# One DMA issue per image of f, earlier copies of images 0 and 1, and one f pair and the attention product ahead of the first taps, in a fused convolution and attention kernel

## The chip, the cores and the metric

The kernel runs on one core of one Trainium2 chip. The metric is the device time of one execution in microseconds (us). Five engines work side by side on a core, each through its own queue in order: TensorE (PE in the profile; its weight loads are PEld), VectorE (DVE), ScalarE (ACT), GpSimd (POOL) and SyncE (SP), which here issues nearly all DMA transfers. They wait for one another through semaphores.

## The reference

For x of 16 images with 256 channels of 32 x 32 pixels, in float32:

```python
x = x + conv_block(_gn(x))      # _gn: group norm, 32 groups of 8 channels
x = x + attention(_gn(x))

# conv_block, cut
f  = relu(einsum('nchw,oc->nohw', x, cw) + conv_b)                  # 256 -> 64 channels
g  = relu(einsum('nc,oc->no', x.mean((2, 3)), cw) + conv_b)         # same weights on the pixel means
K_img = g[:, :, None] * wk + conv_kernel_b                          # 5 x 5 taps per image and channel
gk = relu(k_w0 * K_img + k_w1 * K_img.mean(0) + k_b)                # likewise gk2, 3 x 3
y1 = depthwise_conv(f, gk) + adap_bias                              # 5 x 5
y2 = depthwise_conv(f, gk2, dilation 2) + atrous_bias               # 3 x 3
out = einsum('nchw,oc->nohw', concat(y1, y2), fuse_w) + fuse_b      # 128 -> 256 channels

# attention: blocks of 8 x 8 with a halo of 4; every key that lies inside the image is masked with the
# same large negative number, so a block whose 16 x 16 window lies inside gets the mean of its values
```

What is left of the attention for this input shape is small: the four inner 8 x 8 blocks of every image get one vector, the mean over a 16 x 16 window of the normalised x times Wv and Wout; the outer blocks get the output bias alone.

## The kernel before

All 16 images of x stay in SBUF (tile `xs`). The work goes in two stages that overlap.

**Stage 1, batches of four images.** SyncE loads x, one issue per image (line 202). DVE and ACT compute channel sums, TensorE averages them over groups (`groups(k)`, line 703), DVE and POOL turn that into a reciprocal deviation per channel (`power`, line 301), and POOL multiplies it into the 1x1 weights (`scaled_weights(k)`, line 310). DVE's `scale(k)` (lines 547 to 555) makes the shifts and the pixel means `gm`. TensorE's `f_pair(q)` (line 723) multiplies images 2q and 2q+1 with them, 32 matmuls for two pairs, so 16 for one; ACT's `store_f(q)` (lines 424 to 432, four activations) adds the bias, applies relu and writes f into a slot in SBUF, as 64 channels of eight planes of 153 words. SyncE writes f to a DRAM scratch `fd` (`write_f`, line 214), in four issues per image, each with every fourth channel.

**Stage 2, one image at a time.** SyncE reads each image back from `fd` into one of two buffers `fc[n % 2]`, three copies shifted by one word (`copies(n)`, line 223; 32 rows each); it waits for the image's write and for the taps that used that buffer. TensorE's `taps(n, h)` (line 785, two halves of 32 matmuls) convolves both kernels at once, with weights `wbuf[n % 2]` that POOL (lines 329, 332) and ACT (line 442, four activations per image) make from the scales. DVE transposes the result and orders it (lines 642, 654), TensorE's `fuse(n, c)` (line 797) multiplies it with the fusion weights, DVE adds it to x (line 660), and ACT squares it for the second norm. Chains of two to four images then compute the window means and the inner vectors; POOL adds them and SyncE stores the rows.

**Between the stages**, on TensorE in this order: the first half of f pair 5; a wait for the pixel means `gm`, then the g product (line 746); the second half of f pair 5; two products that spread the scales over the 96 rows of the taps (lines 752, 755), each behind DVE's masked scales (line 609); the bias product (line 757); `shifts(3)` (line 709); and, behind the load of its weights, the attention product Wv by Wout (line 762). DVE copies the spread scales out (lines 616, 629), makes image 0's taps (lines 620 to 626) and finishes the fusion bias (line 631). Then `taps(0)` starts, when copies(0) has landed; f pairs 6 and 7 come between taps(0) and taps(1).

**What sets the order.** Every engine's queue is written out by hand; nothing is scheduled. SyncE's runs: x; the attention weights (lines 205, 207) into `fc[1]`, which is free until copies(1); the writes of images 0 to 5; copies(0); images 6 and 7; a wait for the attention product and the spread scales, which read `fc[1]`; copies(1); images 8 and 9; then per image n copies(n + 2) and, for n below 3, two more writes; from n = 6 on the stores. The slots of f and the odd weight buffer lie in the same tile `reg`, so `taps(1)` on ACT waits until images 4 and 5 are written. PSUM banks are shared too: pairs 0 and 3, the attention product, the spread scales and pair 7 use `pf[0]`; pairs 1, 4 and 6 use `pf[1]`; pairs 2 and 5 use the bank of the odd taps halves.

Of the kernel before, what the change touches and what calls it, by code (L numbers as in the profile page):

```python
# [9 lines left out]
ACT = mybir.ActivationFunctionType  # L10
AX = mybir.AxisListType

N, C, H, W = 16, 256, 32, 32
# [51 lines left out]
def build(nc, x, cw_t, columns, wkv, wout_t, out):  # L65
    with ExitStack() as ctx:
        def sb(name, shape, dt=F32):
            return ctx.enter_context(nc.sbuf_tensor(name, shape, dt))
# [8 lines left out]

        xs = sb("xs", [128, N * NC2 * HW])
        fc = [sb(f"fc{b}", [128, COPY]) for b in range(2)]
        reg = sb("reg", [128, 3072 + WALL])  # L80
        yt = reg[:, 0:1024]
        y2 = [reg[:, 1024:2048], reg[:, 2048:3072]]
        wa = sb("wa", [128, WALL])
# [15 lines left out]
        yb, mixv = cst[:, COLS["yb"]], cst[:, COLS["mix"]]  # L99
        sel, mask16 = cst[0:64, COLS["sel"]], cst[0:64, COLS["mask16"]]  # L100
        wkc, bkc, onc, mask4 = (cst[0:KROWS, COLS[k]] for k in ("wk", "bk", "on", "mask4"))
        wv, wot = fc[1][:, 0:512], fc[1][:, 512:1024]
        sx = fc[1][0:64, 1024:1536].rearrange("p (n g v) -> p n g v", n=N, v=2)

        sm = sb("sm", [128, 622])
        cut = [0]
# [92 lines left out]
        @block.sync  # L199
        def _(sp):  # L200
            for n in range(N):
                sp.dma_start(xs[:, n * NC2 * HW:(n + 1) * NC2 * HW].rearrange("p (c f) -> p c f", c=NC2),  # L202
                             x_v[:, n * NC2:(n + 1) * NC2, :]).then_inc(s_x[n], 16)
            sp.wait_ge(s_fcz, 2)
            sp.dma_start(wv.rearrange("p (k c) -> p k c", k=2),  # L205
                         wkv[C:2 * C, :].rearrange("(k p) c -> p k c", p=128)).then_inc(s_attw, 16)
            sp.dma_start(wot.rearrange("p (k o) -> p k o", k=2),  # L207
                         wout_t.rearrange("(k p) o -> p k o", p=128)).then_inc(s_attw, 16)

            def write_f(n):  # L210
                sp.wait_ge(s_fev, n // 2 + 1)
                m = 64 * (n % 2)
                for c4 in range(4):
                    sp.dma_start(bass.AP(fd, n * IMG + c4 * SPLIT * SET, [[PLANE, GROUPS], [SET, SPLIT], [1, PLANE]]),  # L214
                                 slots[n // 2][m + c4:m + c4 + 61:4, :].rearrange("p (h f) -> p h f", h=SPLIT)
                                 ).then_inc(s_fw[n], 16)

            def copies(n):
                sp.wait_ge(s_fw[n], 64)
                if n >= 2:  # L220
                    sp.wait_ge(s_tap, 2 * (n - 2) + 2)
                for k in range(3):
                    sp.dma_start(fc[n % 2][32 * k:32 * k + 32, LEAD - k:LEAD - k + RUN],  # L223
                                 bass.AP(fd, n * IMG, [[SET, 32], [1, RUN]])).then_inc(s_cp[n % 2], 16)

            def store_rows(n, r0, r1):
                src = xs[:, n * NC2 * HW:(n + 1) * NC2 * HW].rearrange("p (c f) -> p c f", c=NC2)
                sp.dma_start(out_v[:, n * NC2:(n + 1) * NC2, r0 * W:r1 * W],
                             src[:, :, r0 * W:r1 * W]).then_inc(s_store, 16)

            def outer(n):
# [12 lines left out]
            for n in range(6):  # L244
                write_f(n)
            copies(0)
            write_f(6)
            write_f(7)
            sp.wait_ge(s_smm, 2)
            sp.wait_ge(s_atm, 1)  # L250
            copies(1)
            write_f(8)
            write_f(9)
            for n in range(N):
                if n + 2 < N:
                    copies(n + 2)
                if n < 3:
                    write_f(10 + 2 * n)
                    write_f(11 + 2 * n)
                if 6 <= n < 14:  # L260
                    whole(n - 6)
                if n in (12, 13):
                    outer(n - 4)
                if n == 14:
                    inner_rows(8)
                    inner_rows(9)
                    outer(12)
                if n == 15:
                    whole(10)
                    whole(11)  # L270
# [12 lines left out]
        @block.gpsimd  # L283
        def _(pool):
# [17 lines left out]

            def scaled_weights(k):
                pool.wait_ge(s_rstd, k + 1)
                if k == 0:
                    pool.wait_ge(s_cw, 16)
                if k >= 2:
                    pool.wait_ge(s_fmm, 2 * (k - 1))
                r = rstds[k % 2].rearrange("p (j c) -> p j c", c=NC2)
                pool.tensor_tensor(wsc[k % 2], cw[:, :, 0:CM].unsqueeze(2).to_broadcast([128, NC2, BATCH, CM]),  # L310
                                   r.rearrange("p j c -> p c j").unsqueeze(3).to_broadcast([128, NC2, BATCH, CM]),
                                   ALU.mult).then_inc(s_wsc, 1)
# [90 lines left out]
        def _(act):  # L403
# [30 lines left out]
            def taps(n):  # L434
                act.wait_ge(s_pre, n)
                if n == 1:
                    act.wait_ge(s_fw[4], 64)
                    act.wait_ge(s_fw[5], 64)
                if n >= 2:
                    act.wait_ge(s_tap, 2 * (n - 2) + 2)  # L440
                for c4 in range(4):
                    ins = act.activation(wchannel(n, c4), taps_of(n), ACT.Relu, scale=mask4[:, c4:c4 + 1])  # L442
                ins.then_inc(s_w, 1)
# [34 lines left out]
            x_sums(2, 2)  # L478
            for u in range(4):
                x_sums(3, u)  # L480
            for q in range(2, 6):
                store_f(q)
            act.wait_ge(s_p0, 1)
            for c4 in (3,):
                ins = act.activation(wchannel(0, c4), taps_of(0), ACT.Relu, scale=mask4[:, c4:c4 + 1])
            ins.then_inc(s_w0, 1)
            act.wait_ge(s_atm, 1)
            act.activation(at[:, :], pf[0][:, 0:HALF], ACT.Copy, scale=1.0 / KEYS).then_inc(s_at, 1)
            taps(1)
            store_f(6)  # L490
            store_f(7)
            for n in range(1, N):
                if n + 1 < N:
# [13 lines left out]
        def _(dve):  # L507
# [126 lines left out]
            def transpose_half(n, h):  # L634
                i = 2 * n + h
                dve.wait_ge(s_tap, i + 1)
                if n == 0:
                    dve.wait_ge(s_fw[0], 64)
                    dve.wait_ge(s_fw[1], 64)
                else:  # L640
                    dve.wait_ge(s_y2, n)
                dve.transpose(yt[:, h * HALF:(h + 1) * HALF], pt[i % 3]).then_inc(s_t1, 1)  # L642

            def order_image(n):
                dve.wait_ge(s_t1, 2 * n + 2)
                if n < 2:
                    for q in range(2, 6):
                        dve.wait_ge(s_fw[q], 64)
# [48 lines left out]
        def _(pe):  # L697
# [43 lines left out]
            f_pair(4)  # L741
            groups(3)
            f_pair(5, (0,))
            pe.wait_ge(s_gm, BATCHES)
            for c in range(NC2):
                mm = pe.matmul(px[:, 64:64 + N], cw[:, c, :], gm[:, c, :], start=(c == 0), stop=(c == NC2 - 1))
            mm.then_inc(s_gmm, 1)
            f_pair(5, (1,))

            pe.wait_ge(s_sx, 1)  # L750
            flat = fc[1][0:64, 1024:1536]
            pe.matmul(px[0:KROWS, 0:64], sel, flat[:, 0:64], start=True, stop=True).then_inc(s_smm, 1)
            pe.wait_ge(s_sx, 2)
            pe.wait_ge(s_fev, 4)
            pe.matmul(pf[0][0:KROWS, HALF + 64:HW], sel, flat[:, 64:512], start=True, stop=True).then_inc(s_smm, 1)
            for c in range(NC2):
                pe.matmul(pt0[:, 96 + c:97 + c], fw[:, 128 * c:128 * (c + 1)], yb, start=True, stop=True)
            shifts(3)
            pe.wait_ge(s_attw, 32)
            for c in range(NC2):  # L760
                for e in range(NC2):
                    mm = pe.matmul(pf[0][:, C * c:C * (c + 1)], wv[:, C * e + 128 * c:C * e + 128 * (c + 1)],
                                   wot[:, C * e:C * (e + 1)], start=(e == 0), stop=(e == NC2 - 1))
            mm.then_inc(s_atm, 1)

            def taps(n, h):
                i = 2 * n + h
# [53 lines left out]
            for n in range(N):  # L821
# [5 lines left out]
                    if n == when + 1:  # L827
                        attention(k)
                if n == 0:
                    f_pair(6)  # L830
                    f_pair(7)
                else:
                    fuse(n - 1, 0)
                    fuse(n - 1, 1)
# [66 lines left out]
```

## Time and profile before

| | |
|---|---|
| median of 3 runs | 208.42 us (208.18 to 208.69) |
| profiled execution | 209.72 us |
| its span, first to last instruction | 207.6 us |
| mean granted TensorE clock | 0.967 |
| busy share of the span: PE, DVE, ACT, POOL | 79%, 72%, 60%, 43% |
| mean DMA rate | 264 GB/s |

A busy share is an average over stages with different limits. The chain of waits is followed back from the last instruction: at each step to what released it, or to the instruction before it on its engine. PE times are modelled at their ends, and a row of a timeline can merge several instructions (x8). "idle before" names what ended the wait. The granted clock is a share of full speed, 1.00 being 2.4 GHz and 0.50 being 1.2 GHz.

### The profile page before, as it was taken

How to read it: one execution, taken by the hardware profiler on the slowest of the kernel's cores; microseconds unless marked ns; L12 is line 12 of the kernel's file. 1: busy time of each engine (PE TensorE's matmuls, PEld its weight loads, DVE VectorE, ACT ScalarE, POOL GpSimd, SP SyncE). 2: the span in 40 equal slices, each digit the busy share in tenths (PEclk: the TensorE clock that was granted, in tenths of full speed). 3: DMA queues.
4: the chain of work that ended last, by engine and by line, in shares of the span. 5: the costliest groups of instructions: out<-in, count | busy, mean ns of one | idle time of the engine just before them, and what ended most of it. 6: DMA issues, size and time to landing. Idle time of an engine off the chain costs nothing.

```text
span 207.6 us, 3885 instructions
## 1 busy us (share of the span) xinstructions
PE 163.5 (79%) x1374; PEld 102.6 (49%) x1374; DVE 150.1 (72%) x336; ACT 125.2 (60%) x235; POOL 90.1 (43%) x145
## 2 busy tenths in 40 slices
PE   0001796966676999999999999999999999999230
PEld 0000332322246555875775775686676577575030
DVE  0298949887670507898989789989789899799611
ACT  2766679979155064956775775685585686445500
POOL 8703205041339004044146577338857427537540
PEclk9999999999996999999999999999999999999955
DMA  6999999999598996899548487987989998863996
GB/s 218 406 410 410 408 410 410 409 380 213 133 207 190 222 227 161 196 209 222 126 106 184 108 282 180 309 276 186 307 279 253 273 350 211 334 244 153 376 362 223
DMA packets 24466, 54.82 MB, mean 264 GB/s; under 512 B 2560, under 2 KB 14592, under 8 KB 22912
## 3 DMA queue, kind: packets, MB, share of 16 engines
q1 hardware_dynamic: 24032, 54.14, 85.4%
q10 hardware_dynamic: 416, 0.44, 0.8%
q8 instruction: 11, 0.18, 0.4%
q14 instruction: 7, 0.06, 0.1%
HBM read 32.78 MB, written 21.79 MB: 263 GB/s over the span
## 4 chain that ended last, share of the span: by engine, by line
PE 63%; SPq 26%; DMA 4%; DVE 2%; issue 2%; POOL 1%; DVEq 0%; ACT 0%; POOLq 0%
PE pt L785 29%; PE pf L797 28%; SPq L202 14%; SPq L214 9%; DMA fc<-fd 4%; PE pf L723 3%; PE px L817 3%; SPq L207 2%; DVE bs L669 1%; DVE xs L181 1%; DVE xs L660 1%; PE px L808 1%; POOL cw L363 0%; SPq L223 0%; SPq L205 0%
## 5 line engine op out<-in xcount | busy, mean ns | idle before, releaser
L451 ACT ACTIVATE junkt<-xs,sm 128x1024 bf16<-128x1024 f32 x32 | 36.8, 1149 | 39.6 <-DVE xs L660 39.6
L797 PE MATMUL pf<-reg,cst 128*128 128x512 f32 x128 | 59.0, 604 | 0.0
L660 DVE SCALAR_TENSOR_TENSOR xs<-pf,cst,xs 128x1024 f32<-128x1024 f32 x32 | 40.7, 1273 | 8.2 <-PE pf L797 8.2
L642 DVE STREAM_TRANSPOSE reg<-pt 128x512 f32<-128x512 f32 x32 | 22.9, 716 | 20.5 <-PE pt L785 14.3
L329 POOL TENSOR_TENSOR pre<-cst,sv 96x512 f32<-96x512 f32 x15 | 15.8, 1053 | 47.1 <-ACT wa L442 23.1
L418 ACT ACTIVATE wa<-xs 128x1024 bf16<-128x1024 f32 x28 | 29.3, 1051 | 10.6 <-DMA xs<-x_dram 10.6
L797 PEld LDWEIGHTS pf<-reg,cst 128*128 128x128 f32 x128 | 23.0, 190 | 24.4 <-issue 24.4
L785 PE MATMUL pt<-fc,wa 96*64 96x128 f32 x512 | 31.4, 283 | 3.0 <-DMA fc<-fd 3.0
L785 PEld LDWEIGHTS pt<-fc,wa 96*64 96x64 f32 x512 | 29.5, 142 | 8.8 <-issue 5.3
L785 PEld LDWEIGHTS pt<-fc,reg 96*64 96x64 f32 x512 | 27.9, 136 | 5.9 <-issue 5.9
L785 PE MATMUL pt<-fc,reg 96*64 96x128 f32 x512 | 29.7, 273 | 0.0
L181 POOL TENSOR_TENSOR xs<-xs,sm 128x128 f32<-128x128 f32 x58 | 21.3, 401 | 9.7 <-ACT sm L468 9.7
L723 PE MATMUL pf<-xs,junkt 128*64 128x512 f32 x96 | 23.6, 638 | 0.0
L669 DVE TENSOR_REDUCE bs<-xs 128x9 f32<-128x576 f32 x32 | 23.2, 731 | 0.0
L654 DVE STREAM_TRANSPOSE reg<-reg 128x256 f32<-128x256 f32 x64 | 22.8, 414 | 0.5
L520 DVE BATCH_NORM_STATS2 sm<-xs 128x6 f32<-128x512 f32 x36 | 22.5, 681 | 0.2
L442 ACT ACTIVATE reg<-pre,cst 96x512 f32<-96x512 f32 x32 | 21.2, 744 | 1.2 <-POOL pre L332 1.2
L301 POOL TENSOR_TENSOR sm<-sm 128x8 f32<-128x8 f32 x4 | 6.6, 1640 | 33.7 <-DVE sm L545 33.7
L332 POOL TENSOR_TENSOR pre<-pre,sm 96x512 f32<-96x512 f32 x15 | 19.3, 1286 | 1.2
L442 ACT ACTIVATE wa<-pre,cst 96x512 f32<-96x512 f32 x28 | 18.6, 744 | 0.0
L703 PE MATMUL px<-sm,cst 128*128 128x16 f32 x8 | 1.8, 297 | 19.2 <-DVE sm L537 19.2
L723 PEld LDWEIGHTS pf<-xs,junkt 128*64 128x64 f32 x96 | 6.9, 147 | 12.3 <-issue 12.2
(88 smaller groups left out, 125.9 us busy)
## 6 DMA issues: line engine op xcount, KB each, us to landing
xs<-x_dram SPq DMA_DIRECT2D x16, 1024.0 KB, 18.8
fc<-fd SPq DMA_DIRECT2D x48, 306.0 KB, 5.3
out_dram<-xs SPq DMA_DIRECT2D x10, 1024.0 KB, 6.0
out_dram<-xs SPq DMA_DIRECT2D x12, 256.0 KB, 4.3
out_dram<-xs SPq DMA_DIRECT2D x6, 512.0 KB, 3.4
fd<-own SPq DMA_DIRECT2D x40, 76.5 KB, 5.3
fd<-reg SPq DMA_DIRECT2D x24, 76.5 KB, 4.7
cst<-columns_dram ACTq DMA_DIRECT2D x1, 304.0 KB, 4.0
```

The source lines that it names most:

```text
L181: ins = engine.tensor_tensor(rows, rows, add.to_broadcast([128, 8, 2, 8]), ALU.add)
L202: sp.dma_start(xs[:, n * NC2 * HW:(n + 1) * NC2 * HW].rearrange("p (c f) -> p c f", c=NC2), x_v[:, n * NC2:(n + 1) * NC2, :]).then_inc(s_x ...
L418: act.activation(junkl[m % 2], plane(n, c), func, scale=scale, accum_out=dst).then_inc(s_xs, 1)
L442: ins = act.activation(wchannel(n, c4), taps_of(n), ACT.Relu, scale=mask4[:, c4:c4 + 1])
L451: act.activation(junk[m % 2], plane(n, c), ACT.Square, bias=nwb[:, c:c + 1], accum_out=accq[:, 1, m:m + 1]).then_inc(s_sq, 1)
L642: dve.transpose(yt[:, h * HALF:(h + 1) * HALF], pt[i % 3]).then_inc(s_t1, 1)
L654: ins = dve.transpose(dst[:, k], src[:, k])
L660: dve.scalar_tensor_tensor(out=plane(n, c), in0=pf[c][:, :], scalar=fb[:, c:c + 1], in1=plane(n, c), op0=ALU.add, op1=ALU.add, accum_out=r ...
L669: dve.reduce_sum(bs[:, 9 * (m % 16):9 * (m % 16) + 9].rearrange("p (a b) -> p a b", a=3), src, AX.XY).then_inc(s_bs, 1)
L723: mm = pe.matmul(fbank[q][parts, h * HALF:(h + 1) * HALF], wsc[k % 2][:, c, 2 * p + m, :], plane(2 * q + m, c)[:, h * HALF:(h + 1) * HALF] ...
L785: mm = pe.matmul(pt[i % 3][64 * j:64 * j + 64, 128 * s:128 * s + 128], wgroup(n, g, r), rhs, start=(r == 0), stop=(r == 1), tile_position= ...
L797: mm = pe.matmul(pf[c][:, h * HALF:(h + 1) * HALF], fw[:, 128 * c:128 * (c + 1)], y2[n % 2][:, h * HALF:(h + 1) * HALF], start=True, stop= ...
```

## The change

- **f writes.** Each image is written in one issue of 64 channels by eight planes in place of four issues. For that the 64 channels are put in another order on the host (`perm`, applied to the 1x1 weights and biases), and the masks `mask4`, `mask16` and `sel` follow it. The waits on a written image go from 64 to 16.
- **Buffers.** The attention weights and the masked scales move from `fc[1]` to free columns of `reg`, which grows by 96 words; ACT's taps(1), which overwrites them there, waits for the second spread product.
- **SyncE's order.** Images 0 to 3, the two weight loads, copies(0), copies(1), images 4 to 13, copies(2), images 14 and 15, and from there as before. The wait for the attention product and the spread scales ahead of copies(1) is gone.
- **TensorE's order.** First half of pair 5, attention product (with its waits), g product, shifts(3), bias product, first spread, second half of pair 5, second spread, pair 6, taps(0), pair 7, taps(1).
- **ACT's order.** After pair 4's store come the attention matrix, the fourth channel of image 0's taps, the stores of pairs 5 and 6, taps(1), and the store of pair 7.
- **POOL.** The last `scaled_weights` waits until DVE has all pixel means.

```diff
-        wv, wot = fc[1][:, 0:512], fc[1][:, 512:1024]
-        sx = fc[1][0:64, 1024:1536].rearrange("p (n g v) -> p n g v", n=N, v=2)
+        wv, wot = reg[:, 3672:4184], reg[:, 4184:4696]
+        sx = reg[0:64, 4696:5208].rearrange("p (n g v) -> p n g v", n=N, v=2)
...
-                for c4 in range(4):
-                    sp.dma_start(bass.AP(fd, n * IMG + c4 * SPLIT * SET, [[PLANE, GROUPS], [SET, SPLIT], [1, PLANE]]),
-                                 slots[n // 2][m + c4:m + c4 + 61:4, :].rearrange("p (h f) -> p h f", h=SPLIT)
-                                 ).then_inc(s_fw[n], 16)
+                sp.dma_start(bass.AP(fd, n * IMG, [[PLANE, CM], [CM * PLANE, SPLIT], [1, PLANE]]),
+                             slots[n // 2][m:m + CM, :].rearrange("p (h f) -> p h f", h=SPLIT)).then_inc(s_fw[n], 16)
...
-            for n in range(6):
+            for n in range(4):
                 write_f(n)
+            sp.dma_start(wv ...)      # the two weight loads, from ahead of the writes
+            sp.dma_start(wot ...)
+            sp.wait_ge(s_fcz, 2)
             copies(0)
-            write_f(6)
-            write_f(7)
-            sp.wait_ge(s_smm, 2)
-            sp.wait_ge(s_atm, 1)
             copies(1)
-            write_f(8)
-            write_f(9)
+            for n in range(4, 14):
+                write_f(n)
             for n in range(N):
                 if n + 2 < N:
                     copies(n + 2)
-                if n < 3:
-                    write_f(10 + 2 * n)
-                    write_f(11 + 2 * n)
+                if n == 0:
+                    write_f(14)
+                    write_f(15)
...
             def scaled_weights(k):
                 pool.wait_ge(s_rstd, k + 1)
+                if k == BATCHES - 1:
+                    pool.wait_ge(s_gm, BATCHES)
...
                 if n == 1:
-                    act.wait_ge(s_fw[4], 64)
-                    act.wait_ge(s_fw[5], 64)
+                    act.wait_ge(s_fw[4], 16)
+                    act.wait_ge(s_fw[5], 16)
+                    act.wait_ge(s_smm, 2)
...
-            for q in range(2, 6):
+            for q in range(2, 5):
                 store_f(q)
+            act.wait_ge(s_atm, 1)
+            act.activation(at[:, :], pf[0][:, 0:HALF], ACT.Copy, scale=1.0 / KEYS).then_inc(s_at, 1)
             act.wait_ge(s_p0, 1)
...
             ins.then_inc(s_w0, 1)
-            act.wait_ge(s_atm, 1)
-            act.activation(at[:, :], pf[0][:, 0:HALF], ACT.Copy, scale=1.0 / KEYS).then_inc(s_at, 1)
+            store_f(5)
+            store_f(6)
             taps(1)
-            store_f(6)
             store_f(7)
...
             f_pair(5, (0,))
+            pe.wait_ge(s_attw, 32)
+            pe.wait_ge(s_fev, 4)
+            (attention product)
             pe.wait_ge(s_gm, BATCHES)
             (g product)
-            f_pair(5, (1,))
-            (first spread, second spread, bias product)
             shifts(3)
-            pe.wait_ge(s_attw, 32)
-            (attention product)
+            (bias product, first spread)
+            f_pair(5, (1,))
+            (second spread)
+            f_pair(6)
...
                 if n == 0:
-                    f_pair(6)
                     f_pair(7)
```

## Rows read from the trace of the kernel before

**Rows 1.** The page: its span, and the chain that ended last by engine.

```profile
span 207.6 us, 3885 instructions
...
PE 63%; SPq 26%; DMA 4%; DVE 2%; issue 2%; POOL 1%; DVEq 0%; ACT 0%; POOLq 0%
```

**Rows 2.** The chain in order of time: start us, us, what.

```profile
55.40 0.58 SPq L223
...
56.49 7.35 DMA fc<-fd
...
69.27 6.87 PE pf L723 x32
...
79.64 3.63 PE pf L797 x8
83.27 3.65 PE pt L785 x64
...
191.31 1.83 PE pf L797 x4
```

**Rows 3.** Timeline of PE: start us, us, instruction, idle before it.

```profile
50.29 1.94 PE L723 MATMUL pt<-xs,junkt 128*64 128x512 f32 x8
54.30 0.62 PE L746 MATMUL px<-sm,cw 128*128 128x16 f32 x4 [2.07 <-DVE sm L555]
...
56.71 0.38 PE L752 MATMUL px<-fc,cst 64*96 64x64 f32 x2
57.03 0.99 PE L755 MATMUL pf<-fc,cst 64*96 64x448 f32 x2
57.95 0.61 PE L757 MATMUL pt<-cst 128*128 128x1 f32 x4
...
58.86 1.97 PE L762 MATMUL pf<-fc 128*128 128x256 f32 x8
63.88 5.38 PE L785 MATMUL pt<-fc,wa 96*64 96x128 f32 x64 [3.05 <-DMA fc<-fd]
```

**Rows 4.** Windows: PE, PEld, DVE, ACT, POOL busy (x), PEclk, DMA share, GB/s.

```profile
46.00:48.00 2.00, 2.00 (x12) 0.57 (x8) 1.94 (x5) 1.94 (x3) 0.00 (x0) 1.00 1.16 301
...
54.00:56.00 2.00, 1.70 (x10) 1.01 (x12) 1.15 (x7) 0.00 (x0) 0.02 (x1) 1.00 0.40 118
...
63.90:67.40 3.50, 3.50 (x36) 3.50 (x38) 0.00 (x0) 1.35 (x3) 3.06 (x3) 0.54 0.95 194
```

**Rows 5.** Timeline of ACT, DVE and POOL before and around the first taps.

```profile
34.07 0.16 DVE L553 TENSOR_TENSOR sm<-sm 128x8 f32<-128x8 f32 x1
...
46.06 1.06 ACT L418 ACTIVATE wa<-xs 128x1024 bf16<-128x1024 f32 x1 [0.39 <-DMA xs<-x_dram]
...
50.65 0.51 ACT L431 ACTIVATE own<-pf,sm 128x256 f32<-128x256 f32 x1
...
52.97 1.05 POOL L310 TENSOR_TENSOR junkt<-cw,sm 128x512 f32<-128x512 f32 x1
53.01 1.03 DVE L553 TENSOR_TENSOR sm<-sm 128x8 f32<-128x8 f32 x1
...
60.02 0.61 DVE L629 COPY sv<-pf 96x448 f32<-96x448 f32 x1
...
61.05 0.16 DVE L631 TENSOR_TENSOR cst<-pt,cst 128x2 f32<-128x2 f32 x1
...
62.62 2.63 ACT L442 ACTIVATE reg<-pre,cst 96x512 f32<-96x512 f32 x4 [1.15 <-POOL pre L332]
```

**Rows 6.** Sources of issues: ns min/median/max; last line, copies to landing.

```profile
L202 SPq DMA_DIRECT2D xs<-x_dram x16: 438/2234/5354, 0.7 to 26.6; - x16
...
L214 SPq DMA_DIRECT2D fd<-reg x24: 597/600/2371, 35.5 to 54.8; - x24
...
L223 SPq DMA_DIRECT2D fc<-fd x48: 302/422/1547, 55.4 to 170.2; - x48
...
DMA to landing us min/median/max: 3.5/5.3/7.3
```

More of the change, by code:

```diff
@@ L79, in build @@
         fc = [sb(f"fc{b}", [128, COPY]) for b in range(2)]
-        reg = sb("reg", [128, 3072 + WALL])
+        reg = sb("reg", [128, 3072 + WALL + 96])
         yt = reg[:, 0:1024]
@@ L203, in _ @@
                              x_v[:, n * NC2:(n + 1) * NC2, :]).then_inc(s_x[n], 16)
[L204 to L208, printed above, removed]
             def write_f(n):
@@ L212, in write_f @@
                 m = 64 * (n % 2)
-                for c4 in range(4):
-                    sp.dma_start(bass.AP(fd, n * IMG + c4 * SPLIT * SET, [[PLANE, GROUPS], [SET, SPLIT], [1, PLANE]]),
-                                 slots[n // 2][m + c4:m + c4 + 61:4, :].rearrange("p (h f) -> p h f", h=SPLIT)
-                                 ).then_inc(s_fw[n], 16)
+                sp.dma_start(bass.AP(fd, n * IMG, [[PLANE, CM], [CM * PLANE, SPLIT], [1, PLANE]]),
+                             slots[n // 2][m:m + CM, :].rearrange("p (h f) -> p h f", h=SPLIT)).then_inc(s_fw[n], 16)
             def copies(n):
-                sp.wait_ge(s_fw[n], 64)
+                sp.wait_ge(s_fw[n], 16)
                 if n >= 2:
@@ L242, in inner_rows @@
                 store_rows(n, IN0, IN1)
-            for n in range(6):
+            for n in range(4):
                 write_f(n)
+            sp.dma_start(wv.rearrange("p (k c) -> p k c", k=2),
+                         wkv[C:2 * C, :].rearrange("(k p) c -> p k c", p=128)).then_inc(s_attw, 16)
+            sp.dma_start(wot.rearrange("p (k o) -> p k o", k=2),
+                         wout_t.rearrange("(k p) o -> p k o", p=128)).then_inc(s_attw, 16)
+            sp.wait_ge(s_fcz, 2)
             copies(0)
-            write_f(6)
-            write_f(7)
-            sp.wait_ge(s_smm, 2)
-            sp.wait_ge(s_atm, 1)
             copies(1)
-            write_f(8)
-            write_f(9)
+            for n in range(4, 14):
+                write_f(n)
             for n in range(N):
@@ L637, in transpose_half @@
                 if n == 0:
-                    dve.wait_ge(s_fw[0], 64)
-                    dve.wait_ge(s_fw[1], 64)
+                    dve.wait_ge(s_fw[0], 16)
+                    dve.wait_ge(s_fw[1], 16)
                 else:
@@ L647, in order_image @@
                     for q in range(2, 6):
-                        dve.wait_ge(s_fw[q], 64)
+                        dve.wait_ge(s_fw[q], 16)
                 else:
@@ L743, in _ @@
             f_pair(5, (0,))
[L744 to L747, printed above, removed]
-            f_pair(5, (1,))
[L750 to L753, printed above, removed]
-            pe.wait_ge(s_fev, 4)
[L755 to L758, printed above, removed]
-            pe.wait_ge(s_attw, 32)
+            pe.wait_ge(s_attw, 32)
+            pe.wait_ge(s_fev, 4)
             for c in range(NC2):
@@ L764, in _ @@
             mm.then_inc(s_atm, 1)
+            pe.wait_ge(s_gm, BATCHES)
+            for c in range(NC2):
+                mm = pe.matmul(px[:, 64:64 + N], cw[:, c, :], gm[:, c, :], start=(c == 0), stop=(c == NC2 - 1))
+            mm.then_inc(s_gmm, 1)
+            shifts(3)
+            for c in range(NC2):
+                pe.matmul(pt0[:, 96 + c:97 + c], fw[:, 128 * c:128 * (c + 1)], yb, start=True, stop=True)
+            pe.wait_ge(s_sx, 1)
+            flat = reg[0:64, 4696:5208]
+            pe.matmul(px[0:KROWS, 0:64], sel, flat[:, 0:64], start=True, stop=True).then_inc(s_smm, 1)
+            f_pair(5, (1,))
+            pe.wait_ge(s_sx, 2)
+            pe.matmul(pf[0][0:KROWS, HALF + 64:HW], sel, flat[:, 64:512], start=True, stop=True).then_inc(s_smm, 1)
+            f_pair(6)
             def taps(n, h):
@@ L853 @@
             for e in range(6):
-                p = 32 * (e // 2) + 8 * c4 + 2 * ph + e % 2
+                p = 32 * (e // 2) + 8 * ph + 4 * (e % 2) + c4
                 mask4[p, c4] = 1.0
@@ L867 @@
     mask16 = np.zeros((128, GROUPS), np.float32)
-    for ch in range(CM):
-        mask16[ch, ch // 4] = 1.0
-        for p in range(KROWS):
-            if p % 32 // 8 == ch % 4:
-                sel[ch, p] = 1.0
+    for q in range(CM):
+        mask16[q, q % GROUPS] = 1.0
+        sel[q, q // GROUPS:KROWS:4] = 1.0
+    perm = 4 * (np.arange(CM) % GROUPS) + np.arange(CM) // GROUPS
     group_mean = (row[:, None] // GROUP == row[None, :] // GROUP).astype(np.float32) / GROUP
@@ L880 @@
                           a["L0_conv_conv_k2_w"].reshape(-1), a["L0_conv_conv_k2_b"]])
-    conv_b = a["L0_conv_conv_b"].reshape(CM, 1)
-    cw_t = a["L0_conv_conv_w"].reshape(CM, C).T
+    conv_b = a["L0_conv_conv_b"][perm].reshape(CM, 1)
+    cw_t = a["L0_conv_conv_w"].reshape(CM, C)[perm].T
     parts = {"gmat": group_mean, "fw": fw_t, "sel": sel, "mask16": mask16, "wk": wk.reshape(128, -1),
```

## The prediction

> **What bounds the kernel now.** I read the page first, then the chain of waits, the timeline around the chain's one long transfer, the windows there, and the sources of the DMA issues. The profiled execution took 209.72 us: a span of 207.6 [rows 1] and 2.12 around it; the median of the runs is 208.42, 1.30 (0.6%) less. I sum on the span and carry the difference over to the median.
>
> The page gives TensorE 63% of the chain and SyncE's queue 26% [rows 1]. In order of time [rows 2] SyncE's part lies first: it issues without a pause up to the first image's copies from 55.40, a transfer of 7.35 us follows, and TensorE's taps(0) starts at 63.88. From there TensorE is the chain, piece after piece without a gap, until 193.15: taps(0), the f pairs 6 and 7 (6.87 us), taps(1), then one fuse and one taps per image. So whatever leaves TensorE's queue behind 63.88, or lets that point come sooner, shortens the end one for one, as long as nothing else gets in front of TensorE.
>
> Ahead of 63.88 TensorE is idle twice: 2.07 us at 52.23 (waiting for the pixel means) and 3.05 us at 60.83, where the releaser is the copy of f [rows 3]. After the second gap the granted clock averages 0.54 over 3.5 us [rows 4], so nearly all of that stretch ran at the lower of its two levels, 1.2 GHz, and taps(0) takes 5.38 us where the taps of later images take 3.65 [rows 2, 3]. After the first gap, from 54 to 56, the clock stayed at 1.00 [rows 4].
>
> **The change, part by part.**
>
> *f pair 6 ahead of taps(0).* It goes from between taps(0) and taps(1) to before taps(0). The pair of pairs took 6.87 us for 32 matmuls [rows 2], so 16 take 3.44. Behind taps(0): -3.44. Ahead of it the price is in the next sum.
>
> *When TensorE reaches taps(0).* The half pair ends at 50.29 + 1.94 = 52.23 [rows 3]. The attention product (1.97) fits there: its bank is free at 51.16, when the fourth pair's store ends [rows 5], and it ends at 54.20. So it fills the first gap. The pixel means were ready by about 54.25; one of their DVE steps took 1.03 beside a POOL multiplication, against 0.16 in an earlier batch [rows 5]. The new POOL wait parts the two, so the means come some 0.8 earlier, and the g product starts at 54.20 instead of 54.30. POOL's waiting multiplication ends near 54.7 and only pair 6 needs it, five us later; behind it POOL has nothing due before the first taps. From g product to the first spread of scales was 56.71 - 54.30 = 2.41, DVE's chain [rows 3]; the bias product and shifts(3), 57.95 to 58.86 by their starts, hide there. So the first spread is at 56.6, the second half of pair 5 from 56.9 to 58.9 (1.94), the second spread takes 0.92 (57.03 to 57.95) to 59.8, and pair 6 ends at 59.8 + 3.44 = 63.2, against 63.88: -0.6. DVE's last input to taps(0) is the fusion bias: from its copy of the second spread to that bias it took 60.02 to 61.21 [rows 5], so from 59.9 it is ready at 61.1, two us ahead of need. The weights of image 0 depend on the first spread alone, which comes 0.1 sooner than before.
>
> *Clock.* With no gap ahead of it, taps(0) costs the 3.65 of later images: 5.38 - 3.65, so -1.73.
>
> *ACT.* It stores pairs 5 and 6 before taps(1). A store is at most four activations of 0.51 [rows 5], 2.04. From 63.2: pair 6 stored by 65.3, taps(1) (2.63 [rows 5]) by 67.9; TensorE wants it at 63.2 + 3.65 + 3.44 = 70.3. Cost 0, with 2.4 to spare.
>
> *SyncE: first images and weights.* Four issues an image become one. Images 0 to 3 and the two weights go behind x, whose last image has landed by 46.06 [rows 5]. By their shapes (64 x 8 x 153 and 2 x 128 x 512 words) four images are 1.25 MB and the weights 0.52; just after that point the queue moved 301 GB/s, nearly all f writes [rows 4]: 4.2 + 1.7 us, weights landed by 52.0. TensorE wants them at 52.23, in order, with the means behind them. So the delay is 0 at best (a gain is excluded: the half pair ends no sooner). At worst one issue of an image holds SyncE as long as its four of 0.60 [rows 6], 2.4: two images after 46.06, two weight issues of 0.44 and the shortest landing of a copy, 3.5 [rows 6], give 54.8: +2.6. I take +0.4, nearer the low end, because the next paragraph's row argues for short issues.
>
> *SyncE: what an issue costs.* No row has an issue of 512 pieces (64 channels by 8). The nearest: 128 pieces 0.60, x with 256 pieces 0.44 at its shortest, copies with 32 pieces 0.30 to 0.42 [rows 6]. The larger is not the longer. Bounds 0.30 to 2.4 an image; I take 0.8. In 54 to 56 the DMA engines were 40% busy while SyncE issued end to end [rows 4], so the engines can take more than SyncE gave. The Trainium skill (Perfetto Trace Analysis, What "DMA-bound" means) says that an issue's profiled window is descriptor generation; the rows at 32, 128 and 256 pieces don't bear out a window that grows with the count. By that rule the sum would be rival 1's, without it the one below.
>
> *SyncE: what stands behind.* copies(0) and (1) now precede images 4 to 13. SyncE is through with the weights some 2 us before they land, at about 50; from there copies(0) lands at the latest three issues of 0.42 and 7.3 [rows 6] later, at 58.6, before 63.2, and copies(1), a few us behind it, has until 70.3. Then ten images are issued ahead of copies(2). TensorE wants taps(2) at 63.6 + 3.65 + 3.44 + 3.65 + 3.63 = 78.0; copies(2) needs three issues of 0.42 and 5.3 to land [rows 6], so SyncE must reach it by 71.4. From 53 that leaves 18 for ten images: free below 1.8 an image. Images 12 and 13 wait for pair 6's store (65.3), which still fits. Images 14 and 15 stand ahead of copies(3), which has another 7 us. Cost 0.
>
> *The rest.* Moving the buffers from fc to reg and waits of 16 for 64 cost nothing: same bytes, same producers. TensorE's loop from taps(1) on is unchanged, and images written sooner leave it less DMA traffic.
>
> **Sum.** -3.44 - 1.73 - 0.6 + 0.4 = -5.4: span 202.2, profiled 204.3, median **203.0 us**. What is late next: TensorE itself, from 52.2 to the tail.
>
> **Rivals.**
>
> 1. *A whole image's issue holds SyncE as long as its four did* (2.4). Place: SyncE's queue between copies(1) and copies(2). Weights 2.6 late; SyncE reaches the ten images at 46.1 + 4.8 + 0.9 + 2.6 = 54.4, copies(2) at 78.4, landed at 85.0, where TensorE wants it at 63.2 + 2.6 + 14.4 = 80.2: a stall of 4.8, which is longer than the 3.05 after which the clock fell, so 1.73 more. -5.8 + 2.6 + 4.8 + 1.7 = +3.3: about 211.7, slower. It decides from about 2.2 us an image; below 1.8 nothing of it is left. For it: same bytes and pieces. Against: rows 6. Chance 0.11.
>
> 2. *Weights late alone.* The attention product, moved to the front, stalls TensorE and everything behind it by 2 to 2.6, sometimes past the gap after which the clock fell (+1.73). -5.8 + 2 = 204.6 up to -5.8 + 2.6 + 1.4 = 206.6. For it: TensorE is in order and the margin is 0.2 us. Against: 301 GB/s. Chance 0.15.
>
> 3. *The loop gives it back*, the edit not doing what it says for the end: transfers, busy most of the time, bound the images in place of TensorE. 205 to 208.4. Against: in the chain the loop has no DMA piece [rows 2]. Chance 0.09.
>
> If copies(0) still came at 63.88, pair 6 would cover the wait and only the 0.6 would go; that lies inside the forecast.
>
> **How the numbers follow.** Forecast 0.65, with a range of its own of 202.2 to 203.9; rivals 0.11, 0.15, 0.09. From 202.2 to 206.6 lie nearly all of the forecast, rival 2 and a part of rival 3, about 0.8. Outside lie rival 1 and the rest of 3. A measurement tells about 0.2% (0.4 us) from no change. Faster by more: forecast, rival 2 and most of 3, 0.86; within: 0.03; slower: 0.11.
>
> **What would show it.** Right: L214-type issues once an image and near 0.8; taps(0) near 63.2 released by TensorE's own queue with 64 matmuls in 3.65 at clock 1.00; attention product at 52.2; taps(1) near 70.7, behind one f pair alone. Wrong: TensorE idle on the weights at 52, issues above 1.8, taps(2) released by a copy, or a clock below 1.00 before 70.

## The result, and the profile after

The changed kernel takes 212.01 us (median of 4, 210.47 to 212.96), the kernel before 208.56 beside it: ratio 1.0158, 95% interval 1.0113 to 1.0203. The prediction was 203.0 with a range of 202.2 to 206.6: wrong in sign. The profiled execution took 211.79 us, its span is 209.9 (before: 209.72 and 207.6). Executions of one kernel differ by up to 3% here, and the profiled ones of three runs below (e1, e8, e11) were among the longest of their kernel, so of these the rows are read for what waits for what, and the times come from the comparison.

The chain of waits of the changed kernel from SyncE's weight load on (start us, us, what), which answers to [rows 2]:

```profile
46.33 11.14 DMA reg<-wout_t_dram
...
57.51 1.99 PE pf L745 x8
...
61.81 2.62 PE pt L720 x8
64.43 1.74 PE pf L760 x2
66.17 5.31 PE pf L720 x16
71.48 3.50 PE pt L782 x64
74.98 3.44 PE pf L720 x11
```

The one long transfer in the chain is no longer image 0's copies but the second half of the attention weights. They land at 57.47, and the attention product (line 745), which stands next in TensorE's queue, starts at 57.51, 5.3 us after the 52.23 of [rows 3] at which TensorE was to take them up. From there TensorE is the chain to the end, as before, but slowly at first: second half of pair 5, second spread and pair 6 take 2.62, 1.74 and 5.31 us where 1.94, 0.92 and 3.44 were put down. taps(0) starts at 71.3 to 71.5. Behind it all is as predicted: taps(0) in 3.50, one pair in 3.44, and taps(1) in 3.50.

TensorE in the timeline of the changed kernel (start, duration, instruction, idle before it), which answers to [rows 3]:

```profile
53.04 1.94 PE L720 MATMUL pt<-xs,junkt 128*64 128x512 f32 x8
57.51 1.99 PE L745 MATMUL pf<-reg 128*128 128x256 f32 x8 [2.53 <-DMA reg<-wout_t_dram]
```

And SyncE in the same timeline:

```profile
31.15 13.25 SPq L207 DMA_DIRECT2D fd<-reg  x4
44.44 1.84 SPq L238 DMA_DIRECT2D reg<-wkv_dram  x1
46.33 1.02 SPq L240 DMA_DIRECT2D reg<-wout_t_dram  x1
48.52 4.03 SPq L215 DMA_DIRECT2D fc<-fd  x6
53.91 20.47 SPq L207 DMA_DIRECT2D fd<-own  x8
75.08 2.45 SPq L215 DMA_DIRECT2D fc<-fd  x3
```

The first stage ran 2.75 us late in this execution (the half pair at 53.04 for 50.29), which costs nothing: TensorE still waits 2.53 for the weights behind it. SyncE issues images 0 to 3, the two weights, the six parts of copies 0 and 1, then ten images. The row of images 6 to 13 spans 20.47 us, but SyncE does not issue all that time: it also waits for ACT to store f. The waits of the whole run (us in total, times, longest us), and the row of images 12 and 13 alone:

```profile
SPq L207 <- ACT own L426: 8.1, 4, 4.6
...
73.12 1.25 SPq L207 DMA_DIRECT2D fd<-own  x2
```

The longest of these waits, 4.6 us, stands ahead of image 12: pair 6, late with the weights, was stored only at 73.1. Without the waits the eight issues take 14.9 us, 1.9 each, the longest 5.49. And copies(2), at 75.08, follows the end of taps(0) at 74.98, whose buffer it overwrites, not the writes.

Its windows (PE, PEld, DVE, ACT, POOL busy (x), granted clock, DMA share, GB/s), which answer to [rows 4]:

```profile
48.00:50.00 2.00, 2.00 (x12) 0.67 (x10) 1.87 (x6) 2.00 (x8) 0.00 (x0) 1.00 1.22 139
50.00:52.00 2.00, 1.12 (x6) 0.14 (x2) 1.93 (x6) 2.00 (x7) 0.00 (x0) 1.00 1.20 128
...
64.00:66.00 2.00, 2.00 (x4) 0.39 (x2) 0.83 (x3) 1.84 (x5) 1.05 (x1) 0.50 1.20 228
```

Two things are to be seen. The DMA engines are full (share above 1) and move 139 and 128 GB/s where I had counted on 301. And the clock is down ahead of taps(0) instead of in it: 0.70, 0.50, 0.50 and 0.60 in the four windows from 62 to 70, 1.00 in the next. The sum fits: the weights are 5.3 later than 52.2, the stretch from attention product to taps(0) takes 13.8 in place of 11.0, so 8.1 is lost on a gain of 5.8: +2.3, and 207.6 + 2.3 = 209.9.

### The profile page after: what moved, and what is told of

It is laid out like the page before. It is cut to its first block, busy times and chain, and to the rows that moved or that the text cites. A ratio compares the mean times of both kernels' runs of the same rounds, so it can differ in the third digit from the quotient of the medians.

```text
span 209.9 us, 3838 instructions
## 1 busy us (share of the span) xinstructions
PE 167.4 (80%) x1374; PEld 102.3 (49%) x1374; DVE 149.3 (71%) x336; ACT 125.3 (60%) x235; POOL 90.1 (43%) x145
## 4 chain that ended last, share of the span: by engine, by line
PE 72%; DMA 9%; DVE 8%; SPq 5%; issue 1%; POOL 1%; ACT 1%; DVEq 0%; ACTq 0%; POOLq 0%
PE pt L782 28%; PE pf L794 27%; PE pf L720 9%; DMA reg<-wout_t_dram 5%; SPq L207 4%; DMA cw<-cw_t_dram 4%; DVE sm L517 4%; PE px L814 3%; PE pt L720 1%; PE pf L745 1%; SPq L238 1%; PE pf L760 1%; DVE bs L666 1%; DVE xs L657 1%; DVE xs L181 1%
## 5 line engine op out<-in xcount | busy, mean ns | idle before, releaser
L782 PEld LDWEIGHTS pt<-fc,wa 96*64 96x64 f32 x512 | 27.9, 136 | 5.9 <-issue 5.9
L782 PE MATMUL pt<-fc,wa 96*64 96x128 f32 x512 | 29.7, 273 | 0.0
L720 PE MATMUL pf<-xs,junkt 128*64 128x512 f32 x96 | 26.5, 699 | 0.0
L720 PEld LDWEIGHTS pf<-xs,junkt 128*64 128x64 f32 x96 | 7.4, 160 | 15.2 <-issue 15.1
```

The costliest lines, as they stand in the source:

```text
L720: mm = pe.matmul(fbank[q][parts, h * HALF:(h + 1) * HALF], wsc[k % 2][:, c, 2 * p + m, :], plane(2 * q + m, c)[:, h * HALF:(h + 1) * HALF] ...
L782: mm = pe.matmul(pt[i % 3][64 * j:64 * j + 64, 128 * s:128 * s + 128], wgroup(n, g, r), rhs, start=(r == 0), stop=(r == 1), tile_position= ...
```

## The experiments

Theory T: the weights, now behind four images, land late and the clock falls after that; rivals: the new order on TensorE costs by itself (R), or the new layout in DRAM is slow to write (L). Times are compared with the kernel before on the same chip in the same rounds, by ratio and interval. The expectations are in us for a kernel before of 208.4; in the three groups of rounds (e1 to e4, e5 to e8, e9 to e11) its median was 209.7, 210.7 and 209.3. Where an expectation speaks of rings, it means the queues of transfers that are issued and not yet done.

**e1, the weights first.** The two weight loads go back right behind x:

```diff
+            (the two weight loads)
             for n in range(4):
                 write_f(n)
-            (the two weight loads)
             sp.wait_ge(s_fcz, 2)
```

> The changed kernel with one thing undone: the two attention weight loads go right behind x, ahead of the writes of f, as in the kernel before; all else stays changed. Theory T (slow writes delay the weights): a whole-image write moves at 130 to 140 GB/s, so the weights behind four of them land at 57.5 and TensorE stalls on them; in front they land by 48, the attention product starts at 52 to 55, the clock stays at 1.00 up to taps(0), which starts at 63 to 66: 203 to 206 us. Rival R (the new order on TensorE is what costs, wherever the weights stand): the stall moves to another wait, taps(0) still near 71: 210 to 213.

Measured: 207.67 us, ratio 0.9936 (0.9888 to 0.9985). TensorE in its timeline:

```profile
51.92 1.99 PE L745 MATMUL pf<-reg 128*128 128x256 f32 x8
...
64.07 3.68 PE L782 MATMUL pt<-fc,wa 96*64 96x128 f32 x64
...
82.08 6.39 PE L782 MATMUL pt<-fc,wa 96*64 96x128 f32 x64 [3.77 <-DMA fc<-fd]
```

Of its chain, the stretch ahead of taps(2):

```profile
69.59 1.74 SPq L215
...
71.84 10.20 DMA fc<-fd
```

The attention product starts at 51.92 and taps(0) at 64.07: R falls, and 2.2% of the time is won back. But T's 203 to 206 was missed too, because a second wait comes out: taps(2) waits 3.77 us for copies(2), which SyncE reaches at 69.59, behind ten writes (the eight of images 6 to 13 held it for 15.11 us, without a wait between them), and whose last part takes 10.20 us to land (median 5.3 before [rows 6]). The prediction had given SyncE until 71.4, so the landing, not the issue, is what is late. After the wait the taps run at the low clock, 6.39 for 3.65.

**e2, four issues.** The changed kernel, the writes in quarters to the same places; waits on 64:

```diff
-                sp.dma_start(bass.AP(fd, n * IMG, [[PLANE, CM], [CM * PLANE, SPLIT], [1, PLANE]]),
-                             slots[n // 2][m:m + CM, :] ...
+                for c4 in range(4):
+                    sp.dma_start(bass.AP(fd, n * IMG + c4 * SET, [[PLANE, GROUPS], [CM * PLANE, SPLIT], [1, PLANE]]),
+                                 slots[n // 2][m + 16 * c4:m + 16 * c4 + 16, :] ...
```

> The changed kernel with each image again written in four issues, now 16 channels in a row each, to the same DRAM places as the single issue (pieces of one channel 39,168 bytes apart). Theory T in the form that the single issue is what makes the writes slow: with four issues the rate from 46 to 52 goes back to 200 GB/s, the weights land near 53 to 55: 204 to 208 us. Rival L (the new places in DRAM make them slow): 130 to 140 GB/s as in the changed kernel, weights near 57: 210 to 213.

Measured: 211.55 us, ratio 1.0135 (1.0031 to 1.0239), as the changed kernel. Lines of its chain:

```profile
48.18 9.24 DMA reg<-wout_t_dram
57.47 3.78 PE pf L747 x8
```

The weights land at 57.47, just as with one issue. So the single issue is not what delays them, and T in that form is out; time and landing are those of rival L. The windows from 48 to 52 show 158 and 156 GB/s at full engines. Whether the layout has a part is for e3 and e7.

**e3, one issue alone.** The kernel before with the channels reordered, `write_f` and its waits as in the change, and nothing else.

> The kernel before with one part of the change alone: reordered channels and one issue per image; the queues' order and the buffers as before. If the issue time on SyncE was what delayed copies(0) (the reading ahead of the prediction), they are issued some 5 us sooner and taps(0) starts near 60: 203 to 206 us. Theory T: six images at 130 to 140 GB/s lie ahead of copies(0) in the rings, 1.9 MB or 14 us from 46 on, so copies(0) is issued no sooner than 55 and lands at 62 to 68: 207 to 213.

Measured: 205.63 us, ratio 0.9872 (0.9825 to 0.9918). Its timeline:

```profile
35.64 15.49 SPq L213 DMA_DIRECT2D fd<-reg  x6
51.17 3.11 SPq L221 DMA_DIRECT2D fc<-fd  x3
54.33 1.26 SPq L213 DMA_DIRECT2D fd<-own  x2
...
61.46 3.73 PE L783 MATMUL pt<-fc,wa 96*64 96x128 f32 x64 [0.52 <-DVE cst L629]
```

copies(0) is issued at 51.17 for 55.40, the gap ahead of taps(0) shrinks to 0.52 and the clock stays at 1.00, so taps(0) takes 3.73. Two images are issued in 1.26 us with few transfers outstanding: 0.6 an image of 512 pieces, as much as 128 pieces took before. 48 to 50 shows 238 GB/s in the new layout, so L is out as well. The first expectation came out, but for taps(0) 1.5 us later than its 60, and T's 207 to 213 did not. This part of the change is a gain by itself.

**e4, weights first and four issues.** Both edits of e1 and e2.

> The changed kernel with both: weights right behind x, and four issues per image. Theory T: neither the weights nor the rate is in the way; SyncE's issue time, 2.4 us an image, comes back, so copies(2) may come late (ten images from about 53 to 77, taps(2) wanted near 78): 203 to 210 us. Rival R: 210 to 213.

Measured: 211.78 us, ratio 1.0148 (1.0061 to 1.0235). The time misses T and lies in R's range, but not by R's mechanism: taps(0) starts at 64.16, as in e1. Here SyncE's issues make copies(2) late: 32 of them from 58.53 on take 16.45 us, SyncE is through at 75.0 where the prediction had given it until 71.4, and taps(2) waits 4.30:

```profile
58.53 16.45 SPq L208 DMA_DIRECT2D fd<-own  x32
...
82.70 6.04 PE L784 MATMUL pt<-fc,wa 96*64 96x128 f32 x64 [4.30 <-DMA fc<-fd]
```

Once copies(2) stands behind ten images, four issues an image cost 4 us more than one (207.67 and 211.78 in the same rounds).

**e5, the writes interleaved.** e1, and:

```diff
-            for n in range(4, 14):
+            for n in range(4, 10):
                 write_f(n)
...
-                if n == 0:
-                    write_f(14)
-                    write_f(15)
+                if n < 3:
+                    write_f(10 + 2 * n)
+                    write_f(11 + 2 * n)
```

> The run with the weights first, and one more part of the change undone: after copies(1) only images 4 to 9 are written, and images 10 to 15 follow two by two behind copies(2), (3) and (4), as in the kernel before. Theory T2 (the ten writes ahead of copies(2) fill the rings, so its landing takes 10 us and TensorE stalls 3.8 us at taps(2) and runs the next one at the low clock): copies(2) lands before 78, no stall, 201 to 203.5 us. Rival B (the same bytes have to pass before the later images anyway): the stall moves to taps(3) or (4), 205 to 208.

Measured: 205.48 us, ratio 0.9791 (0.9696 to 0.9887). The stall at taps(2) is gone and none takes its place, as T2 had it; but 205.48 misses T2's 201 to 203.5 (the ratio makes it 204.1 on the 208.42 of the prediction). It lies in the range of rival B, whose mechanism, a stall at taps(3) or (4), is not there. The windows (columns as above) say where the time is:

```profile
56.00:58.00 2.00, 1.84 (x8) 0.83 (x10) 1.93 (x5) 0.00 (x0) 0.00 (x0) 0.84 1.13 269
58.00:60.00 2.00, 2.00 (x5) 0.39 (x2) 1.52 (x4) 1.37 (x3) 0.37 (x1) 0.50 0.89 199
```

TensorE in its timeline, and from SyncE's the issue of copies(2):

```profile
56.16 0.38 PE L757 MATMUL px<-reg,cst 64*96 64x64 f32 x2 [0.69 <-DVE reg L606]
56.47 2.86 PE L720 MATMUL pt<-xs,junkt 128*64 128x512 f32 x8
59.26 1.81 PE L760 MATMUL pf<-reg,cst 64*96 64x448 f32 x2
61.00 5.21 PE L720 MATMUL pf<-xs,junkt 128*64 128x512 f32 x16
66.04 3.67 PE L782 MATMUL pt<-fc,wa 96*64 96x128 f32 x64
...
80.21 3.73 PE L782 MATMUL pt<-fc,wa 96*64 96x128 f32 x64
...
69.80 1.32 SPq L215 DMA_DIRECT2D fc<-fd  x3
```

copies(2) is issued at 69.80, no sooner than in e1 (69.59), but behind six images in place of ten, and taps(2) at 80.21 waits for nothing. The clock falls between 56 and 58, although from 50.4 on TensorE's longest gap was the 0.69 us ahead of line 757; before the fall it had the attention product and then matmuls of 16, 4, 1 and 64 columns. The three groups at lines 720, 760 and 720 take 9.9 us, where at full clock they take 1.94 + 0.99 + 3.65 = 6.6 (e7 below has them so): 3.3 lost in this execution.

**e6, the order alone.** The kernel before with the order of TensorE, ACT and POOL of the change.

> The kernel before with the other part alone: the order of TensorE, ACT and POOL of the changed kernel; four issues an image, SyncE's order and buffers as before, so the weights are there by 48. Theory P (TensorE's part of the forecast holds): attention product at 52.2, taps(0) at 63.9 with the copies of image 0, 3.65 us long, and 3.44 less behind it: 203 to 205 us. Rival R (the order itself lowers the clock or stalls): 207 to 210.

Measured: 207.63 us, ratio 0.9879 (0.9774 to 0.9985), which lies at the lower end of R's range (the ratio makes it 205.9 on the 208.42 of the prediction, between P and R). In its profile the attention product starts at 52.49, pair 6 is off the way behind taps(0), and the clock is at 0.50 from 58 on, with 2.47, 1.81 and 5.60 for the same three groups; taps(0) starts at 66.29. That is R's lower clock: the order gains, and of the 5.2 us that P counted on (1.73 and 3.44) the profiled execution gives 3.3 back.

**e7, copies after the weights.** The changed kernel with `sp.wait_ge(s_attw, 32)` ahead of copies(0).

> The changed kernel with one wait more: SyncE issues copies(0) only when the weights have landed. Theory M (the copies of images 0 and 1, issued from 48.5 on, share the engines with the last writes and the weights and hold them up): the weights land by 53 to 54.5, 207 to 210 us. Rival W (the four writes alone hold them up): still 56 to 57.5 and the copies later too, 211 to 215.

Measured: 214.79 us, ratio 1.0233 (1.0096 to 1.0371). SyncE, then TensorE in its timeline:

```profile
46.28 0.70 SPq L240 DMA_DIRECT2D reg<-wout_t_dram  x1
53.85 2.67 SPq L215 DMA_DIRECT2D fc<-fd  x6
```

```profile
53.82 1.99 PE L746 MATMUL pf<-reg 128*128 128x256 f32 x8 [1.92 <-DMA reg<-wout_t_dram]
...
58.05 1.94 PE L721 MATMUL pt<-xs,junkt 128*64 128x512 f32 x8
59.92 0.99 PE L761 MATMUL pf<-reg,cst 64*96 64x448 f32 x2
60.84 3.65 PE L721 MATMUL pf<-xs,junkt 128*64 128x512 f32 x16
64.32 3.67 PE L783 MATMUL pt<-fc,wa 96*64 96x128 f32 x64
...
85.89 6.03 PE L783 MATMUL pt<-fc,wa 96*64 96x128 f32 x64 [7.33 <-DMA fc<-fd]
```

M holds for the weights: with the copies held back they land at 53.8, 3.7 us sooner than 57.5 from the same issue time (one profile of each). The time I put on M is wrong all the same, and 214.79 lies in W's range, since the later copies push ten writes and copies(2) back, and taps(2) waits 7.33. How the copies hold the weights up is not shown. By the sizes of the packets in the trace of the changed kernel, the pieces of the copies (9,792 bytes) move only from 53.3 on. The pieces of f (612 bytes) slow down in both runs from 47 on, before any copy is issued, to about half of the 245 to 283 KB that they moved from 46 to 47; in e7 they are back at 201 KB from 49 to 50, in the changed kernel they stay at 136.

**e8, pair 5 whole.** e5, with `f_pair(5)` in one piece ahead of the g product and the attention product behind the spreads; ACT stores pair 5 first.

> The run with the writes interleaved, and on TensorE the gap ahead of the g product filled with the second half of pair 5 in place of the attention product, which comes behind both spreads, just ahead of pair 6; ACT stores pair 5 first. Theory C (the stretch of small matmuls from 52 to 56 is what let the clock fall at 56.5 in the run with the weights first, 1.7 us): clock 1.00 from 50 to 70 and taps(0) near 63: 1 to 2 us less than the run with the writes interleaved. Rival: the clock falls there all the same, equal within 0.5.

Measured: 205.86 us, ratio 0.9796 (0.9694 to 0.9898), equal to e5 (0.9791). The clock falls here too, only later (0.80 in the window from 58 to 60, 0.50 from 60 to 66): the small matmuls still stand together, from 56.4 to 60.8. Its rival came out: moving full-size matmuls ahead of the stretch made no difference to the time.

**e9, half of pair 6 in the wait.** e5, and:

```diff
+            f_pair(6, (0,))
             pe.wait_ge(s_sx, 1)
...
-            f_pair(6)
+            f_pair(6, (1,))
```

> The run with the writes interleaved, with the first half of f pair 6 moved into TensorE's wait for DVE's masked scales (54.9 to 56.2 there, between the bias product and the first spread). Theory C (the clock fell at 56.8 because TensorE had little but small matmuls and a wait since 52; 3.3 us): full matmuls in that stretch keep it at 1.00, and the wait of 1.3 is used as well, taps(0) near 61.5 in place of 66.0: 200 to 202 us. Rival F (the fall has nothing to do with that stretch): only the 1.3 go, 203.5 to 205.

Measured: 203.66 us, ratio 0.9763 (0.9715 to 0.9812); the span of the profiled execution is 201.0. This is less than either kernel, but the interval overlaps that of e5, and the time misses C's 200 to 202 and lies in the range of F. One window, and TensorE in the timeline:

```profile
58.00:60.00 2.00, 2.00 (x10) 0.52 (x6) 1.93 (x4) 0.68 (x2) 0.00 (x0) 1.00 0.94 230
```

```profile
55.33 1.94 PE L720 MATMUL pf<-xs,junkt 128*64 128x512 f32 x8
...
62.06 3.67 PE L783 MATMUL pt<-fc,wa 96*64 96x128 f32 x64
```

taps(0) starts at 62.06, 4.0 sooner than in the profiled execution of e5, and the clock is 1.00 in every window from 46 to 72. So this one execution has the clock as C had it, while the time does not decide between C and F.

**e10, discarded matmuls in the wait.** e5 with three matmuls of 512 columns in the same place, whose result nobody reads:

```diff
+            pe.wait_ge(s_fev, 5)
+            for c in (0, 1, 0):
+                pe.matmul(pf[1][LO, 0:HALF], cw[:, c, 0:CM], plane(12, c)[:, 0:HALF], start=True, stop=True)
             pe.wait_ge(s_sx, 1)
```

> The run with the writes interleaved, with three added matmuls of full size (1.3 us, their result is thrown away) in the same wait, and nothing moved. Theory C: the clock holds, taps(0) near 62.8, 202 to 203 us although TensorE does more. Rival F: the clock falls as before, 205 to 206.

Measured: 205.63 us, ratio 0.9853 (0.9809 to 0.9896). They took 2.79 us, not 1.3 (six matmul records from 55.33 to 58.05), which delays the first spread, and yet taps(0) starts sooner than in e5, because the groups behind run at full clock (the last line is the window from 58 to 60):

```profile
55.33 2.79 PE L757 MATMUL pf<-xs,cw 128*64 128x512 f32 x6
...
64.63 3.67 PE L785 MATMUL pt<-fc,wa 96*64 96x128 f32 x64
...
58.00:60.00 2.00, 2.00 (x11) 0.73 (x10) 1.46 (x3) 0.00 (x0) 0.00 (x0) 1.00 1.05 223
```

As to the clock C holds in this execution, since work was only added. As to the time, 205.63 lies in the range of F, and the run is no better than e5: whatever the clock gave, the added work took.

**e11, interleaved with the weights late.** The changed kernel with e5's second edit alone.

> The changed kernel with the writes interleaved, but the weights still behind images 0 to 3. Theory: the two waits stand one behind the other, and the first hides the second: the weights land at 57 as before, taps(0) at 70 to 71, and copies(2) were in time already there, so 210 to 212, as the changed kernel. Rival: the writes of images 10 to 15, now later, take load off the rings around 50 to 57 and the weights land sooner: 206 to 209.

Measured: 214.12 us beside 209.29, from four executions of 210.49 to 214.60, too far apart for an interval. The weights release the attention product at 57.24, taps(0) starts at 72.72, and taps(2) waits for nothing. So the rival (weights sooner) falls, and with late weights copies(2) is in time with either order of the writes. Whether the two orders take the same time is not shown.

## Why the prediction was wrong

**The step that failed** is "SyncE: first images and weights": "just after that point the queue moved 301 GB/s, nearly all f writes [...] weights landed by 52.0", at worst +2.6. They landed at 57.5, and TensorE took them up 5.3 late. Two things went wrong in it.

The first is the rate. The reading of the window from 46 to 48 is right:

```profile
DMA packets 1065, 0.60 MB, mean 301 GB/s; under 512 B 114, under 2 KB 1065, under 8 KB 1065
```

Of its 601 KB, 554 are pieces of 612 bytes (153 words), which only f has. But I carried this rate over all 1.77 MB, and it did not last. The next window of the same kernel has the engines just as full of f and moves a third less:

```profile
48.00:50.00 2.00, 0.41 (x3) 0.04 (x1) 1.77 (x9) 2.00 (x8) 0.00 (x0) 1.00 1.18 200
```

At 200 GB/s four images take 6.3 us instead of 4.2; with 1.7 for the weights that is 54.1, near the 53.8 of e7. The second is the copies of images 0 and 1, which go with the other 3.7. I had them land early and cost nothing, but they are issued from 48.5, as soon as image 0 is written, and e7, which holds them back, has the weights 3.7 sooner; by what path they delay them stays open. So rival 2 was the right place, at twice its price and with the clock on top. (Its upper end of 206.6 adds 1.4 for the clock where it names 1.73; with 1.73 it is 207.0.)

**The clock term.** "With no gap ahead of it, taps(0) costs the 3.65": true for taps(0), but I reckoned with a fall behind a long idle gap alone. With the new order it fell ahead of the dense work in the profiles of e1, e4, e5 and e6, where no gap from 50.7 on was longer than 0.7 us. The three groups behind the first spread then took 1.65 us more than at full clock (e1, e4) or 3.3 (e5, e6). In e7, with the same order and more idle time, it did not fall. So the order alone does not decide it, and what does stays open. With full-size matmuls in the stretch it stayed up (e9, e10), in one profiled execution of each. That they are the reason is not shown: the profiled execution of e5 was the longest of its four, with a span of 204.6 and a mean clock of 0.957 where the others have 202.7 to 202.9 and 0.967 to 0.969, and three of e9's six have no more than that, 0.965 to 0.968.

**SyncE's ten images.** "Free below 1.8 an image": the issue itself is 0.6, below my 0.8, and rival 1's mechanism, an issue that costs as much as four, did not happen. That 211.7 was near the result is chance. The rule of the Trainium skill (Perfetto Trace Analysis, What "DMA-bound" means), that an issue's window is descriptor generation, differs from the traces here: the same 512 pieces took 0.59 to 6.05 us in the changed kernel (last section), so the window holds a wait as well. But rival 1's place, SyncE's queue ahead of copies(2), was right. With many transfers outstanding a write holds SyncE longer than its 0.6: 1.9 each for images 6 to 13, in the changed kernel and in e1 (15.11). The bound on SyncE still held in e1: its ten images took 1.64 each, from 53.08 to 69.49, and copies(2) was issued ahead of 71.4. The term that failed is the landing of 5.3: behind ten writes the last part of copies(2) took 10.20. In the changed kernel late weights hide it, and there copies(2) waited for taps(0); take the late weights away and it costs 3.77 us and a stretch at the low clock (e1 against e5: 0.9936 and 0.9791).

**What held.** Pair 6 behind taps(0) -3.44; taps(0) at full clock; from attention product to taps(0) 10.5 us at full clock (e7), against 11.0 in my sum; the attention product in the first gap where the weights are there (51.92 in e1, 52.24 in e5); ACT's and POOL's moves cost nothing that the chains show; the loop did not give anything back (rival 3). With the two queue orders mended and the clock at 1.00, the profiled execution of e9 comes to a span of 201.0, 1.2 below the forecast's 202.2.

Part by part: one issue alone -1.3% (e3), the order of the engines alone -1.2% (e6), and both with the weights first and the writes of images 10 to 15 spread between the copies -2.1% (e5). The changed kernel differs from e5 in SyncE's order alone, and that turns -2.1% into +1.6%. The three gains come from different rounds, and their intervals overlap, so how they add up is not shown.

## What to carry to other kernels

When a transfer is moved behind others in one queue, count all bytes that will be in flight between its issue and its landing, later issues included, and take the rate from several windows of the same traffic: here f moved at 277 GB/s in one window and at 200 in the next. Ask of an issue that is moved forward, and of a removed wait, what it lets loose: here 1.9 MB of copies came right behind the weights. A row that merges eight issues can hold waits for another engine; look at the single issues before the span is put down to the queue. And when TensorE's work is regrouped, look at the granted clock ahead of the dense part, in more than one execution.

## What the runs showed of the hardware

- The granted clock fell to 0.50 with no idle gap over 0.69 us between 50.4 and the fall (e5, between 56 and 58), behind the attention product and a run of matmuls of a few columns. With three full-size matmuls there, which fill that gap too, it stayed at 1.00 in the profiled execution (e10); in e7 it stayed at 1.00 without them.
- With the same order on TensorE up to there, executions differ in it: sixteen matmuls of f in the first stage, from 35 us on, took 4.99 us in the profile of the changed kernel and 5.06 in e8, and 3.65 in the other profiles.
- An issue's time on SyncE does not follow the number of pieces: 128 pieces from every fourth partition 0.60 us (median, kernel before), 128 from adjacent partitions 0.45 (median, e2), 512 from adjacent partitions 0.6 (e3, with few transfers outstanding). With much outstanding the same issue of 512 pieces took up to 6.05 us, as the sources of the changed kernel's issues show (ns min/median/max):

```profile
L207 SPq DMA_DIRECT2D fd<-reg x6: 586/1086/6048, 31.2 to 53.2; - x6
```

- Writes of f ran the 16 engines full at 139 GB/s (changed kernel, 48 to 50; 276 of 277 KB are pieces of f), where f moved at 277 in the kernel before (46 to 48) and x alone at 410. What makes them so slow was not taken apart.
